# Two attentions and two feed-forward layers on one core: the ones column beside V, and where V starts in its row

## The reference, cut to what matters

```
# attention A: 16 heads of 64, no mask, 2048 queries by 2048 keys
scores = einsum('bnhd,bmhd->bhnm', Q, K) * (SCALE * adaptive_scale)
w      = softmax(scores, axis=-1)
attn   = einsum('bhnm,bmhd->bnhd', w, V)
y      = layernorm(x + attn @ Wo.T + bo) * gamma + beta

# attention B: 8 heads of 128, rotary, causal mask (keys after the query left out)
s = einsum('bihd,bjhd->bhij', rope(q), rope(k)) / 128
p = softmax(s - 1e30 * (i < j), axis=-1)
o = einsum('bhij,bjhd->bihd', p, v)
r = einsum('bihd,hdm->bim', o, w_ao)
```

## Time and profile before

| what | value |
|---|---|
| median of 3 executions | 1926.67 us |
| lowest and highest | 1925.68 and 1926.8 us |
| profiled execution, span from first to last instruction | 1927.3 us |
| mean granted TensorE clock in it | 0.987 of full speed |
| matmuls | 23471 |
| of these, weights-by-V in A (L1600, L1601, L1603) | 3 x 4096 |
| and in B (L1859, L1861, L1863) | 3 x 1088 |

### The profile page before, as it was taken

The page is one execution under the profiler, slowest core; times in us unless marked ns, Lnnn a source line. Parts: engine busy times, 40 slices in busy tenths (PEclk is TensorE's granted clock), DMA queues, the critical chain, the costliest instruction groups (busy, mean ns, idle before and its releaser), DMA issues.

```text
span 1927.3 us, 55726 instructions
## 1 busy us (share of the span) xinstructions
PE 1854.3 (96%) x23471; PEld 1256.4 (65%) x23471; DVE 1443.6 (75%) x2647; ACT 1548.5 (80%) x1921; POOL 1597.5 (83%) x1025
## 2 busy tenths in 40 slices
PE   4899999999999999999999998779999999999998
PEld 3566666666666666666666665547777777767766
DVE  7798878878878878878878875566767767767652
ACT  4799999999999999999999999646666666666664
POOL 3899999999999999999999999358688787787752
PEclk8999999999999999999999999889999999999999
DMA  6101100100100100100100100100000000000000
GB/s 148 35 11 26 34 15 22 35 17 20 35 19 18 35 19 18 35 19 17 35 23 14 35 2 2 55 1 2 2 1 2 2 2 2 2 1 1 2 2 23
DMA packets 45034, 37.96 MB, mean 20 GB/s; under 512 B 8304, under 2 KB 44144, under 8 KB 44528
## 3 DMA queue, kind: packets, MB, share of 16 engines
q1 hardware_dynamic: 44304, 34.00, 7.0%
q10 hardware_dynamic: 480, 0.39, 0.1%
HBM read 8.15 MB, written 1.05 MB: 5 GB/s over the span
## 4 chain that ended last, share of the span: by engine, by line
PE 87%; DVE 4%; POOL 3%; issue 3%; ACT 2%; DMA 0%; SPq 0%; POOLq 0%; DVEq 0%; ACTq 0%
PE ST L1639 11%; PE ST L1640 11%; PE RING L1520 7%; PE OO L1601 6%; PE OO L1603 6%; PE OO L1600 6%; PE OO L1520 4%; PE ST L1832 3%; PE ST L1838 3%; PE ST L1837 3%; PE ST L1839 3%; POOL PBUF L704 2%; PE OO L1859 2%; PE OO L1861 2%; PE OO L1863 2%
## 5 line engine op out<-in xcount | busy, mean ns | idle before, releaser
L620 POOL TENSOR_TENSOR PAB<-PR,PAB 128x1024 f16<-128x1024 f32 x342 | 724.3, 2134 | 42.3 <-ACT PAB L799 42.2
L799 ACT ACTIVATE PAB<-ST,exp_scale 128x1024 f16<-128x1024 f32 x512 | 567.6, 1109 | 0.0
L1104 DVE TENSOR_REDUCE maxes<-RING 128x1 f32<-128x512 f32 x661 | 439.6, 684 | 122.6 <-PE RING L1520 118.2
L1600 PE MATMUL OO<-VP,PAB 128*128 128x66 f16 x4096 | 446.6, 192 | 2.9 <-POOL PAB L620 2.9
L1601 PE MATMUL OO<-VP,PAB 128*128 128x64 f16 x4096 | 447.1, 193 | 0.0
L1603 PE MATMUL OO<-VP,PAB 128*128 128x66 f16 x4096 | 445.1, 192 | 0.0
L797 ACT ACTIVATE PR<-ST,exp_scale 128x1024 f32<-128x1024 f32 x342 | 381.9, 1117 | 64.7 <-PE ST L1640 61.8
L1600 PEld LDWEIGHTS OO<-VP,PAB 128*128 128x128 f16 x4096 | 380.2, 96 | 78.3 <-issue 15.5
L1601 PEld LDWEIGHTS OO<-VP,PAB 128*128 128x128 f16 x4096 | 377.0, 97 | 60.6
L1639 PE MATMUL ST<-QL,KH 128*128 128x512 f16 x1024 | 388.6, 380 | 2.0 <-DVE QH L1116 1.0
L1640 PE MATMUL ST<-QH,KL 128*128 128x512 f16 x1024 | 388.8, 380 | 0.0
(11 more groups left out here) (319 smaller groups left out, 4027.8 us busy)
## 6 DMA issues: line engine op xcount, KB each, us to landing
KH<-HS SPq DMA_DIRECT2D x124, 64.0 KB, 2.0
QL<-HS SPq DMA_DIRECT2D x64, 64.0 KB, 2.0
QL<-LS SPq DMA_DIRECT2D x64, 64.0 KB, 2.0
QH<-HS SPq DMA_DIRECT2D x64, 64.0 KB, 2.0
KL<-LS SPq DMA_DIRECT2D x62, 64.0 KB, 2.0
X<-in_L_attn_a_x SPq DMA_DIRECT2D x4, 256.0 KB, 4.2
SHARED<-in_rope_cos SPq DMA_DIRECT2D x1, 1024.0 KB, 5.2
SHARED<-in_rope_sin SPq DMA_DIRECT2D x1, 1024.0 KB, 7.3
```

The source lines that it names most:

```text
L620: pool.tensor_tensor(PB[:, s, :], PRA[g % PR_SLOTS], PA[:, s, :], ALU.subtract).then_inc(p_low_ready, 1)
L799: act.activation(PA[:, step % SLOTS_A, :], ST[step % 2][:, :], ACT.Exp, scale=scale).then_inc(sa.exps, 1)
L1104: dve.reduce_max(maxes[:, i // BLOCKS, i % BLOCKS:i % BLOCKS + 1], bank[:, :], X_AXIS).then_inc(sa.ring_taken, 1)
L1600: pe.matmul(o, high, v[:, 0:V2_AT], start=(m == 0 and qt == 0), stop=False, skip_group_check=True)
```

## The change

One column of ones instead of two in both attentions. The high part of V starts at column 1 and the low part at column 65 (A) or 129 (B). The matmuls that take ones and V high have 65 and 129 columns; the ones with V low keep 64 and 128. Accumulators lie 65 and 129 fp32 columns apart. One unused column is put at the end of the row (V_END and VB_END are where V ends), so that rows stay 130 and 258 columns long.

```diff
-V1_AT = 2
+V1_AT = 1
 V2_AT = V1_AT + DA
-VCOL = V2_AT + DA
+V_END = V2_AT + DA
+VCOL = V_END + 1
...
-V1B_AT = 2
+V1B_AT = 1
 V2B_AT = V1B_AT + DB
-VB = V2B_AT + DB
+VB_END = V2B_AT + DB
+VB = VB_END + 1
...
-                dve.tensor_tensor(vp[:, :, V2_AT:VCOL], vf, vp[:, :, V1_AT:V2_AT], ALU.subtract
+                dve.tensor_tensor(vp[:, :, V2_AT:V_END], vf, vp[:, :, V1_AT:V2_AT], ALU.subtract
...
-                dve.tensor_tensor(v[:, :, V2B_AT:VB], bank[:, :].rearrange("p (t c) -> p t c", c=DB),
+                dve.tensor_tensor(v[:, :, V2B_AT:VB_END], bank[:, :].rearrange("p (t c) -> p t c", c=DB),
...
-                    pe.matmul(o[:, V1_AT:V2_AT], high, v[:, V2_AT:VCOL], start=False, stop=False,
+                    pe.matmul(o[:, V1_AT:V2_AT], high, v[:, V2_AT:V_END], start=False, stop=False,
...
-                    pe.matmul(o[:, V1B_AT:V2B_AT], high, v[:, V2B_AT:VB], start=False, stop=False,
+                    pe.matmul(o[:, V1B_AT:V2B_AT], high, v[:, V2B_AT:VB_END], start=False, stop=False,
```

## The result

| | before | after |
|---|---|---|
| median of 6 executions each | 1926.74 us | 1932.9 us |
| lowest and highest | 1925.68 and 1929.32 | 1931.77 and 1935.06 |
| ratio, 95% interval | | 1.0028, 1.0016 to 1.0039 |
| profiled span | 1927.3 us | 1930.0 us |

The change makes the kernel slower by 0.28%, some 5.4 us by the ratio (3.1 to 7.5); the two medians stand 6.2 us apart. The forecast was 1.6 us faster.

A forecast was written before the change was run, and what follows sets the result against it. TensorE was taken as the bound in both attentions. Columns saved (4.3 us) minus alignment lost (2.7 us) gave 1.6 us less: 1926.67 - 1.6 = 1925.1 us, called "the same", range 1920 to 1942.

The forecast's parts named there:

- The bound: In both attentions TensorE was taken as the bound, so time added to or saved at its matmuls moves the end.
- One column from two of every three matmuls, at 0.417 ns: Weights-by-V matmuls one column narrower: A 3.4 us and B 0.9 us less.
- I take that for 2, 6, 10 and 14: V low starting 2 bytes off a 4-byte word was taken to cost the same 2 ns as starts 4, 8, 12 off.
- the upper bound: For V low's odd start: one more tick pair (0.83 ns) for each matmul, 4.3 us lost.
- The lost quarter: V low's aligned quarter of key tiles loses its alignment: A 2.1 us and B 0.6 us more.
- Odd places in PSUM, taken as 0: Half of the outputs starting at an odd fp32 column were taken to cost nothing; upper bound 2 ns each.
- The rival that priced it at 2 ns each: Odd output starts in PSUM cost what unaligned SBUF starts do: 16.1 us, ending at 1941.2; chance 0.17.
- The rival of pairs: TensorE moves two columns at a time, so 65 cost 66 and odd V low costs more: 7.0 us slower, 1933.7; chance 0.22.
- with odd starts free: Bound for V low's start: 2 ns less for all 5184 matmuls, a further 12.8 us gained.
- the rival of the vanished stall: Odd places avoid the 2 ns at V low's matmuls: 12.8 us faster, 1913.9; chance 0.12, gone or partly gone.
- The other engines: VectorE's and ScalarE's writes of V, 691 and 599 ns, were costed at 0; were they doubled, 10 us at most.

The follow-up runs named there:

- the map of widths: The kernel with 16-byte rows, its two full-row matmuls narrowed by m % 8 columns at key tile m; 1905.89 us, one execution.
- the kernel with 16-byte rows: Kernel before with V low at column 72 (A) or 136 (B), rows of 136 and 264 columns; 1923.58 us, 0.998 of before.
- the three maps: Kernel before with starts shifted through 16 bytes by key tile: full rows and low part, low part alone, full rows alone; 1930.47, 1923.44, 1928.12 us.

## Why the prediction was wrong

**The bound** was right. TensorE's waits stayed the same to 0.1 us, and the time went with its matmuls.

**"One column from two of every three matmuls, at 0.417 ns", 4.3 us:** this is the step that failed. The slope of 0.42 ns a column was measured between even widths alone, which the text said and the rival used. The width by itself gives 1.0002 of before, and the map of widths shows steps of 0.8 ns every second column. The term is 0. The loads are not the reason: a matmul of 128 columns takes 55.8 ns in that map, and the spacing still shrinks from 64 columns to 60. (So the rule of the Trainium skill's "TensorE: Matmul & The Clock Gate", section "Back-to-back issue gap", weighed in the prediction, had this term at 0 too, but by loads that set some 81 ns at 128 columns, with which the runs don't agree.)

**"I take that for 2, 6, 10 and 14"** of the odd start of V low: it costs one pair, 0.8 ns, on top, and I had that as the upper bound, 4.3 us. Groups went from 336.4 to 339.6, 0.8 ns for each of four matmuls; the same came out in B alone, with the start moved by one column, as 170.0 against 169.2.

**The lost quarter, 2.7 us:** the sign was right and A was sized too small. The 256 groups went from 328.2 to 342.0, 13.8 ns, where I had 8.2 (and 8.2 + 3.3 = 11.5 with the pair). In B 3.6 ns against 2.6 + 0.8. The 2.05 ns of A was a net of two things that I read as one: the gap behind the matmul with V low was 4.5 ns shorter in the aligned tiles (28.5 against 33.1), and lumps stood elsewhere in them (31.6 against 29.2 behind the last matmul of a run). After the change both are gone (34.1 and 29.2). The reason I gave for it, a start off 16 bytes, is not what the runs show: a start 2 bytes off, away from the row just read, costs a pair and no more in B.

**Odd places in PSUM, taken as 0:** wrong by itself, since a run of three in B with one odd start in PSUM costs 0.7 ns more when all else is even, but harmless here, where it hides behind the odd start in SBUF. The rival that priced it at 2 ns each, 16 us, is ruled out: with the accumulators 66 apart the full rows write from even columns and nothing came back (1.0032), and an odd start of the matmul with V low was seen at 0.8 ns in B.

**The whole.** With the measured prices: A 768 x 3.2 + 256 x 13.8 ns = 6.0 us, B 864 x 0.8 + 224 x 3.6 = 1.5 us, 7.5 us in all; measured 5.4 (3.1 to 7.5), and 5.3 of A's 6.0 can be seen in the profile. The rival of pairs had 7.0. I had given it 0.22 against 0.42 with nothing in the trace for or against either: every width and start in this kernel is even, and that fact deserved an even split at least. One bound of the sum was added up wrongly, too: with odd starts free, 4096 x 2.05 + 1088 x 2.6 = 11.2 us more would have been gained on top of the forecast, not 12.8, which is the whole of it as the rival of the vanished stall has it. The forecast does not rest on it.

**The other engines** were right: VectorE's writes went from 691 to 694 ns, ScalarE's from 599 to 607.

```profile
L874 ACT ACTIVATE PAB<-RING 128x512 f16<-128x512 f32 x23 | 13.9, 607 | 1.7 <-PE RING L1764 1.5
L1089 DVE TENSOR_TENSOR VP<-RING,VP 128x512 f16<-128x512 f32 x18 | 12.5, 694 | 0.6
```

## What to carry to other kernels

In a dense stream of short matmuls, count the columns of an fp16 operand in SBUF and of the fp32 output in PSUM in pairs: an odd width costs the next even one, and an even width from an odd start costs one pair more, about 0.8 ns at full clock. Taking away a single column of ones is worth nothing, and moving thousands of small matmuls to odd starts costs time (5.4 us for 5184 here, the lost alignment included). Where a second operand is read right behind the first in the same row, leave a gap so that it starts at a multiple of 16 bytes: that gave 0.2% here (0.998, 0.9971 to 0.9989) for six columns of SBUF a row.

## What the runs showed of the hardware that was not expected

- The matmul with V low costs 2.6 ns more in B (2 in A, net of the lumps) when it starts off 16 bytes right behind the row just read. Off 16 bytes alone does not set the price: one column past a multiple, away from that row, costs a pair only (170.0 ns a run), two columns past 0.7 ns, but six columns past 2.4 ns. Which of the start in the line, the line shared with the read before, and the order of reads sets the price stays open; the three maps leave more than one reading.
- A saving at one matmul of the stream can come back as gaps about 6 ns longer at others: in the kernel with 16-byte rows groups of A fell by 4.2 ns on the mean, which is 4.3 us over 1024 groups, and A's products got 1.5 us shorter. In the map of widths such gaps stand in every group at 66 and 65 columns, two of them, and all but never at 64 and below.
- An odd start in SBUF and one in PSUM in the same matmul cost one pair together, not two (172.3 and 172.4 ns a run at query tile 1, with an even and an odd start in PSUM).
